# A second attention that also does the scales, the choice of experts and the normalised rows, in three portions of batches

## The reference

```
h = concat(patch_embedding(x), txt)                       # 32 x 96 x 192
h = h + attention12(layernorm(h))                         # 12 heads
h = h + soft_moe(layernorm(h))                            # 64 slots, fc1 768, gelu, fc2
h = h + attention1(layernorm(h))                          # 1 head, rotary q and k, causal
h = h + moe(layernorm(h))

def moe(x):            # x is flattened to 3072 x 192, 8 experts, top 2
    logits = x @ Wr
    topw, topi = top_k(logits, 2);  topw = softmax(topw)
    hidden = relu(x @ W1[e] + b1[e])                      # 192 -> 768
    y = hidden @ W2[e] + b2[e]                            # 768 -> 192
    return sum over the two experts of topw * y
```

## Time and profile before

| | us |
|---|---|
| median of 3 runs | 986.27 (982.88 to 988.9) |
| profiled execution | 982.65 |
| its span, first to last instruction | 980.9 |
| TensorE busy | 790.7 (81%) |
| VectorE busy | 546.9 (56%) |
| ScalarE busy | 437.7 (45%) |
| GpSimd busy | 301.3 (31%) |
| mean granted TensorE clock | 0.865 of full |

### The profile page before, as it was taken

The page is one execution under the profiler, slowest core; times in us unless marked ns, Lnnn a source line. Parts: engine busy times, 40 slices in busy tenths (PEclk is TensorE's granted clock), DMA queues, the critical chain, the costliest instruction groups (busy, mean ns, idle before and its releaser), DMA issues. The chain is left out here.

```text
span 980.9 us, 22531 instructions
## 1 busy us (share of the span) xinstructions
PE 790.7 (81%) x7454; PEld 651.8 (66%) x7455; DVE 546.9 (56%) x1512; ACT 437.7 (45%) x1056; POOL 301.3 (31%) x310
## 2 busy tenths in 40 slices
PE   3489999999779866665457999964189999999993
PEld 2368888888668533333344888852189999999993
DVE  1727777777875121111172766758356666666662
ACT  4345766667453311111003798645234444444441
POOL 1321112110034000000101587620165655555552
PEclk9758999999975787777775999975589999999997
DMA  9393000000000599999608300008613333323331
GB/s 270 90 417 152 3 0 0 0 0 1 1 2 2 238 428 424 426 428 425 263 12 341 145 1 0 1 30 128 118 39 53 52 53 51 53 47 51 53 49 19
DMA packets 39784, 119.35 MB, mean 122 GB/s; under 512 B 11130, under 2 KB 30108, under 8 KB 35260
## 3 DMA queue, kind: packets, MB, share of 16 engines
q1 hardware_dynamic: 28520, 104.98, 29.2%
q0 software_dynamic: 10848, 12.76, 8.2%
q10 hardware_dynamic: 356, 0.82, 0.3%
HBM read 105.75 MB, written 12.56 MB: 121 GB/s over the span
## 5 line engine op out<-in xcount | busy, mean ns | idle before, releaser
L1741 POOL DMA_INDIRECT out_h<-x_ys,idx x55 | 87.2, 1586 | 97.7 <-ACT x_ys L1767 74.9
L1873 PE MATMUL psum<-w_pairs,x_h_hi 128*128 x330 | 102.1, 371 | 2.0 <-DVE x_h_lo L1801 1.1
L1875 PE MATMUL psum<-w_pairs,x_h_lo 128*128 x330 | 82.6, 250 | 0.0
L1801 DVE TENSOR_TENSOR x_h_lo<-psum,x_h_hi 128x384 fp32r<-128x384 f32 x110 | 56.2, 553 | 41.9 <-ACT x_h_hi L1762 41.9
L1767 ACT ACTIVATE x_ys<-x_ys,x_cw 128x192 f32<-128x192 f32 x55 | 25.1, 456 | 98.3 <-DVE x_ys L1812 98.3
L1762 ACT ACTIVATE x_h_hi<-psum 128x384 fp32r<-128x384 f32 x110 | 48.0, 489 | 41.6 <-PE psum L1862 41.6
L1873 PEld LDWEIGHTS psum<-w_pairs,x_h_hi 128*128 128x128 f32 x330 | 61.9, 188 | 4.2 <-issue 4.2
L1875 PEld LDWEIGHTS psum<-w_pairs,x_h_lo 128*128 128x128 f32 x330 | 62.9, 191 | 0.0
L1728 POOL DMA_INDIRECT x_xg<-xtab,idx x55 | 55.3, 1005 | 16.6 <-issue 14.6
L478 POOL TENSOR_SCALAR a_xn<-flat,rstd,nmr 96x192 f32<-96x192 f32 x32 | 16.1, 502 | 136.9 <-PE psum L609 136.8
L1115 PE MATMUL psum<-flat,m_yT 64*32 64x384 f32 x576 | 38.0, 609 | 24.8 <-issue 23.5
(11 more groups left out here) (290 smaller groups left out, 2189.4 us busy)
## 6 DMA issues: line engine op xcount, KB each, us to landing
flat<-in_slot_w SPq DMA_DIRECT2D x24, 2304.0 KB, 28.6
flat<-in_moe_w SPq DMA_DIRECT2D x1, 10752.0 KB, 28.6
ring_last<-in_slot_w SPq DMA_DIRECT2D x4, 2304.0 KB, 33.6
m_y<-in_slot_w SPq DMA_DIRECT2D x4, 2304.0 KB, 31.3
flat<-in_x_patches SPq DMA_DIRECT2D x4, 1536.0 KB, 15.1
out_h<-flat SPq DMA_DIRECT2D x1, 2304.0 KB, 12.2
xtab<-flat SPq DMA_DIRECT2D x4, 576.0 KB, 11.8
ytab<-f_y2g SPq DMA_DIRECT2D x28, 48.0 KB, 28.1
```

The costliest lines, as they stand in the source:

```text
L1741: pool.indirect_dma_start(out=A["out"][:, :], out_offset=bass.IndirectOffsetOnAxis(ap=g.idx[:, i:i + 1], axis=0), in_=ys[:, i % 2, :], in_ ...
L1801: v.tensor_tensor(h_lo[:, 3 * n:3 * n + 3, :], b_hT[n], h_hi[:, 3 * n:3 * n + 3, :].bitcast(F32), ALU.subtract).then_inc(s_hl, 1)
L1873: pe.matmul(b_y[u % 2], h_hi[:, k, :], g.w_pairs[:, :, k, bass.ds(e, 1), :].rearrange("p two a d -> p two (a d)"), start=(k == 0), stop=False)
L1875: mm = pe.matmul(b_y[u % 2][:, 1, :], h_lo[:, k, :], g.w_pairs[:, 1, k, bass.ds(e, 1), :].rearrange("p a d -> p (a d)"), start=False, stop ...
```

## The change

In `attention1` every stage keeps its place; `residual` now adds into `g.h` directly, so `hn`, `keep` and its copy are gone. The batches are divided into three portions, 0 to 15, 16 to 27 and 28 to 31. When the statistics of a portion are complete, new stages follow with lags 6 to 10 behind its last batch: `variance` and `scales` (on VectorE, with `root` on ScalarE between them: logarithm and exponential and a Newton step in place of square root and reciprocal), `first_choice`, `second_choice` and `gate_weights` (VectorE, with `ratio` on ScalarE). GpSimd normalises the rows in place (`normalise`, two batches per step for the first portion, three for the second, four for the last) instead of ScalarE in `route`. SyncE writes output and table in eight groups of four batches. The column sums of the router's weights are made at the start. The loops of VectorE and TensorE are written out (`few_steps` for `steps`).

`route` keeps the counts, places and lists. There GpSimd makes the low parts of all eight late pieces; ScalarE makes each high part when its group of the table is written. `expert_tiles` no longer has the late pieces, and its first matmul waits for all of them.

```diff
+            def store_h(n):
+                part = slice(4 * n, 4 * n + 4)
+                sp.wait_ge(s_res, part.stop)
+                sp.dma_start(out_rows[:, part, :], g.h[:, part, :]).then_inc(s_h[n], 16)
+            def store_x(n):
+                part = slice(4 * n, 4 * n + 4)
+                sp.wait_ge(s_xo, part.stop)
+                sp.dma_start(tab_rows[:, part, 0:D], g.h[:, part, :]).then_inc(g.s_tab[n], 16)
+                sp.dma_start(tab_rows[:, part, D:DK], g.h[:, part, 2 * 64:D]).then_inc(g.s_tab[n], 16)
+                sp.wait_ge(s_gates, chunk_of[part.stop - 1] + 1)
+                sp.dma_start(tab_rows[:, part, DK:DK + 3], gates[:, part, :]).then_inc(g.s_gt, 16)
+            for n in range(groups):
+                store_h(n)
+                if n >= groups - 3:
+                    store_x(2 * (n - groups + 3))
+                    store_x(2 * (n - groups + 3) + 1)
+            store_x(groups - 2)
+            store_x(groups - 1)
...
+                v.scalar_tensor_tensor(g.h[:, b, :], b_o, sc[:, i, 3:4], g.h[:, b, :], ALU.mult, ALU.add).then_inc(s_res, 1)
...
+            def variance(n, c):
+                st = g.stats[:, c, :]
+                v.wait_ge(s_st, c.stop)
+                mark(v.tensor_tensor(mean[:, c], st[:, :, 1], st[:, :, 4], ALU.add))
+                mark(v.tensor_tensor(half_diff[:, c], st[:, :, 1], st[:, :, 4], ALU.subtract))
+                link(v.tensor_tensor(var[:, c], st[:, :, 2], st[:, :, 5], ALU.add))
+                mark(v.tensor_tensor(half_diff[:, c], half_diff[:, c], half_diff[:, c], ALU.mult))
+                link(v.tensor_scalar(var[:, c], var[:, c], 1.0 / D, EPS, ALU.mult, ALU.add))
+                v.scalar_tensor_tensor(var[:, c], half_diff[:, c], 0.25, var[:, c], ALU.mult, ALU.add).then_inc(s_var, 1)
+            def scales(n, c):
+                v.wait_ge(s_y, n + 1)
+                link(v.tensor_tensor(newton[:, c], y[:, c], y[:, c], ALU.mult))
+                link(v.tensor_tensor(newton[:, c], newton[:, c], var[:, c], ALU.mult))
+                link(v.tensor_scalar(newton[:, c], newton[:, c], -0.5, 1.5, ALU.mult, ALU.add))
+                link(v.tensor_tensor(g.rstd[:, c], y[:, c], newton[:, c], ALU.mult))
+                v.scalar_tensor_tensor(g.nmr[:, c], mean[:, c], -0.5, g.rstd[:, c], ALU.mult, ALU.mult).then_inc(s_nrm, 1)
...
+            def best(k, src, c):
+                size = c.stop - c.start
+                experts = g.iota[0:T, 0:NE].unsqueeze(1).broadcast_to([T, size, NE])
+                link(v.tensor_reduce(m[:, k, c], src[:, c, :], AX.X, ALU.max))
+                link(v.tensor_tensor(key[:, c, :], src[:, c, :], wide(m[:, k, c], NE), ALU.is_equal))
+                link(v.scalar_tensor_tensor(key[:, c, :], key[:, c, :], -float(NE), experts, ALU.mult, ALU.add))
+                link(v.tensor_reduce(place[:, k, c], key[:, c, :], AX.X, ALU.min))
+                link(v.tensor_tensor(g.oh[:, k, c, :], key[:, c, :], wide(place[:, k, c], NE), ALU.is_equal))
...
+            def first_choice(n, c):
+                v.wait_ge(s_gs, c.stop)
...
+                mark(v.tensor_tensor(lg[:, c, :], lg[:, c, :], wide(g.rstd[:, c], NE), ALU.mult))
+                link(v.tensor_tensor(key[:, c, :], wide(g.nmr[:, c], NE),
+                                     colsum[:, :].unsqueeze(1).broadcast_to([T, c.stop - c.start, NE]), ALU.mult))
+                link(v.tensor_tensor(lg[:, c, :], lg[:, c, :], key[:, c, :], ALU.add))
+                best(0, lg, c)
+            def second_choice(n, c):
+                mark(v.tensor_scalar(gates[:, c, 2], place[:, 0, c], float(NE), None, ALU.add))
+                link(v.scalar_tensor_tensor(lg2[:, c, :], g.oh[:, 0, c, :], -1e30, lg[:, c, :], ALU.mult, ALU.add))
+                best(1, lg2, c)
+                v.tensor_tensor(ex[:, c], m[:, 1, c], m[:, 0, c], ALU.subtract).then_inc(s_d, 1)
+                v.tensor_tensor(g.both[:, c, :], g.oh[:, 0, c, :], g.oh[:, 1, c, :], ALU.add).then_inc(g.s_both, 1)
...
+            def gate_weights(n, c):
+                v.wait_ge(s_ex, n + 1)
+                link(v.tensor_scalar(c0[:, c], ex[:, c], 1.0, None, ALU.add))
+                link(v.reciprocal(c0[:, c], c0[:, c]))
+                link(v.tensor_tensor(gates[:, c, 0], ex[:, c], c0[:, c], ALU.mult))
+                v.tensor_tensor(gates[:, c, 1], c0[:, c], gates[:, c, 0], ALU.subtract).then_inc(s_gates, 1)
...
+            few_steps(B, [(residual, 5), (gate_copy, 7), (statistics, 5), (inverse, 4), (rotate, 2), (soften, 3),
+                          (per_chunk(variance), 6), (per_chunk(scales), 7), (per_chunk(first_choice), 8),
+                          (per_chunk(second_choice), 9), (per_chunk(gate_weights), 10)], UNROLL)
...
-            def keep(b, i):
-                item(pool, s_res, b)
-                pool.tensor_copy(g.h[:, bass.ds(b, 1), :], hn[:, i, :].unsqueeze(1)).then_inc(s_keep, 1)
...
+            def normalise(at, i):
+                for b in turns[at] if at in turns else ():
+                    pool.wait_ge(s_nrm, chunk_of[b] + 1)
+                    pool.wait_ge(s_hTp, b + 1)
+                    pool.wait_ge(s_h[b // 4], 16)
+                    pool.tensor_scalar(g.h[:, b, :], g.h[:, b, :], g.rstd[:, b:b + 1], g.nmr[:, b:b + 1],
+                                       ALU.mult, ALU.add).then_inc(s_xo, 1)
...
-            few_steps(B, [(keep, 5), (add_parts, 2), (split_low, 1)], UNROLL)
...
+                    n, c = chunk_at[b], slice(*chunks[chunk_at[b]])
+                    item(act, s_var, n)
+                    act.activation(lnv[:, c], g.lnt[:, 2, c], ACT.Ln).then_inc(s_lnv, 1)
+                    item(act, s_lnv, n)
+                    act.activation(y[:, c], lnv[:, c], ACT.Exp, scale=-0.5).then_inc(s_y, 1)
...
+            few_steps(B, [(x_copy, 1), (r_copy, 3), (root, 7), (ratio, 10), (p_copy, 4), (h_copy, 6), (v_copy, 2), (norm_input, 0),
+                          (split_high, 0), (exponent, 3), (tail_top, 3)],
...
-            steps(pe, B, [(gate, 7), (transpose_x, 1), (project, 2), (transpose_qk, 3), (transpose_p, 4), (turn_h, 6),
-                          (project_v, 2), (score, 3), (attend, 4)])
...
+            few_steps(B, [(gate, 7), (transpose_x, 1), (project, 2), (transpose_qk, 3), (transpose_p, 4), (turn_h, 6),
+                          (project_v, 2), (score, 3), (attend, 4)], UNROLL)
...
-            sp.dma_start(A["out"][0:NTOK, :].rearrange("(b t) d -> t b d", t=T), g.h[:, :, :]).then_inc(s_h, 16)
...
+            for n in range(B // 4):
+                sp.wait_ge(g.s_tab[n], 32)
+            sp.wait_ge(g.s_gt, 16 * (B // 4))
...
+            for n, (_, full, hi, lo) in enumerate(g.late_pieces):
+                pool.wait_ge(g.s_hi, len(g.pieces) + n + 1)
+                pool.tensor_tensor(lo, full, hi.bitcast(F32), ALU.subtract).then_inc(g.s_lo, 1)
...
-            act.wait_ge(s_d, 1)
-            act.activation(ex[:, :], ex[:, :], ACT.Exp).then_inc(s_ex, 1)
...
-            act.wait_ge(s_h, 16)
-            for b in range(B):
-                act.activation(g.h[:, b, :], g.h[:, b, :], ACT.Identity, scale=g.rstd[:, b:b + 1],
-                               bias=g.nmr[:, b:b + 1]).then_inc(s_norm, 1)
-            act.wait_ge(s_tab, 11 * 16)
-            for _, full, hi, _ in g.late_pieces:
+            for n, (_, full, hi, _) in enumerate(g.late_pieces):
+                act.wait_ge(g.s_tab[n], 32)
                 act.activation(hi, full, ACT.Copy).then_inc(g.s_hi, 1)
...
-            link(v.tensor_tensor(g.lg[:, :, :], g.lg[:, :, :], wide(g.rstd[:, :], NE), ALU.mult))
...
-            pe.wait_ge(s_both, 1)
+            pe.wait_ge(s_ones, 1)
...
-                if t == NX - 1:
-                    for n in on_pool:
...
-            for n in on_vector:
-                v.wait_ge(g.s_hi, n_early + n + 1)
...
-            pe.wait_ge(g.s_lo, n_early)
+            pe.wait_ge(g.s_lo, len(g.pieces) + len(g.late_pieces))
```

## The result

| | before | after |
|---|---|---|
| median, us | 986.33 (982.88 to 988.9, 4 runs) | 1006.11 (1004.71 to 1007.9, 4 runs) |
| ratio of the times | | 1.0207, 95% interval 1.0182 to 1.0232 |
| span of the profiled execution | 980.9 | 1004.4 |
| granted clock, mean | 0.865 | 0.85 |

The changed kernel is slower: the interval of the ratio lies above 1. A second measurement of it, with other kernels on the chip, gave 1006.25 and a ratio of 1.0216 (1.0187 to 1.0245). The forecast was 1001 us, range 980 to 1009. Between the two profiled executions the difference is 23.5 us, between the medians 19.8; the forecast of +17 was made for the profiled one.

What follows compares the result with a forecast made beforehand. TensorE was taken to bound attention and expert tiles, with a nearly idle hand-over between. -7.4 us without conflict plus 24.4 of port waits gave +17: 999.7 profiled, 1003 on the median, 1001 taken, range 980 to 1009.

Steps and rivals of the forecast that it cites:

- forecast of +17: Whole kernel: -7.4 us without conflict plus 24.4 us of waits between VectorE and GpSimd, on the profiled execution.
- Routing: Block after attention: 21.0 us gained without conflict, 11.8 lost as VectorE's list chain waits for GpSimd's eight subtractions.
- The rule itself: VectorE operations with two SBUF inputs and GpSimd operations reading SBUF exclude each other for a whole instruction; +24.4 us together.
- The middle: First portion's stages in mid-attention: 5.4 us without conflict plus 6.6 of VectorE waiting for GpSimd.
- 5.4 without conflict: Middle of the attention: 3.0 us for ScalarE's root with table loads, 2.4 for VectorE's added operations.
- The tail: End of attention, portions two and three: +9.9 us of linked stages without conflict, +6.0 of waits beside GpSimd's rows.
- the +6.0 for GpSimd's rows: Attention tail: VectorE's choices wait beside GpSimd's 12 and 4 normalised rows, three quarters of which meet a waiting operation.
- Opening: Start of the expert tiles: no wait for late pieces and faster first gathers, 2.0 us gained.
- Rival 1: Routing and the choices: VectorE never waits for GpSimd or pays nothing; -7.4 us, 975 to 979; chance 0.20.
- Rival 2: VectorE waits in only one place, attention or routing; about +4.5 us, 988 to 991; chance 0.14.
- Rival 3: End of attention: SyncE's queued transfers, not the engines, hold the table; 999 to 1003 us; chance 0.04.

Runs made afterwards that it cites:

- late_back: Changed kernel with the eight late low parts moved out of routing, back to the opening of the expert tiles; 996.38 us, ratio 1.0103.
- micro: Changed kernel with a test stretch behind its end, each kind of VectorE operation beside each kind of GpSimd operation; its time is no measure.
- lo_paused: Changed kernel with GpSimd making no low parts in attention steps 21 to 25, the eight left in steps 26 to 32; 999.55 us, ratio 1.0134.
- two24: Changed kernel with two portions (24 and 8 batches) instead of three, rows three a step behind the first; 997.49 us, ratio 1.0175.
- final: Changed kernel with portions of 24 and 8 batches, late low parts at tile opening, VectorE reciprocal root, last gates in one transfer; 980.94 us, ratio 0.9961.

## Why the prediction was right

- **Routing, -21.0 without conflict, +11.8 with it.** Right: the chain grew by 12.4, and late_back took them away to within 0.1. The place was not right: the forecast let the waits begin at `pos` and fall on two-input operations, with `r_info` or `r_key` as the sign; they began 1.2 us into the chain, all eight fell on `r_e`, and five of them on copies and one-input operations. That the sum came out so near is in part luck: by the forecast's own rule those five would not have waited.
- **The rule itself.** Right that such an exclusion exists, wrong on who takes part. The forecast rested on x_mine, and for one-input operations on the row of 96x96, which is a reduction. Reductions pass; one-input scalings and copies of 8 elements do not (micro), while the scalings of one element do (L1271). The Trainium skill, "SBUF — State Buffer", section "Who interferes with whom", names besides two-input operations also copies and one-input scalings of VectorE, in modes that take the shared ports, and says that reductions never contend; the forecast used only its first part. On VectorE's side micro agrees with all three (1769, 1724 and 421 ns at most). The section also has any GpSimd instruction that reads SBUF contend with two inputs. Beside the rows, which read one tile, two inputs of 8 elements took 289 ns at most and of 256 elements 611 for 420: less than one row of 507 was lost, so there is contention, but the whole-instruction wait on which the forecast built was not measured.
- **The middle, +12.0.** Too low: +19.0 measured, 14.6 to 19.0 over three executions. The waits were sized well: one operation per burst waits until GpSimd's queue is empty, 7.2 us at the choices and weights (2.12, 2.01, 3.05) against 7.1. The 1.78 at the variance had no term. Nor had the clock, which held 636 to 642 at half speed; after lo_paused the middle was still +8.7, and two24's +9.8 has no wait either, against 5.4 without conflict. How the 3.3 us or more above 5.4 divide between the clock and ScalarE's and VectorE's own added work is open. Five batches took 6.8 to 8.1 us, not three.
- **The tail.** +9.9 without conflict was right (+9.8); the +6.0 for GpSimd's rows did not occur, because rows don't exclude. The errors of middle and tail, +7.0 and -6.1, nearly cancelled.
- **Opening, -2.0.** -0.6: the gather began 0.9 us after the block in place of 1.5, but landed 4.5 us after its start instead of 3.3. Over the seven profiles that open with the late parts already made, the end of the list to that matmul was 13.7 to 15.5 us, over the four edits that open with late pieces still to make 14.7 to 15.7, so the term is hardly to be told from nothing.
- **Rivals.** Rival 1 needed waits under 7.4 us; routing alone had 12.4. Rival 2 needed one place free; both had them. Rival 3: SyncE waited 2.0 us for the table at the start of routing, until 692.5, long before the lists ended.

The sum of +17 came from terms of which two were wrong by 6 to 7 us with opposite signs; that luck brought the number so near. The sign of the result rests on routing and the middle, which the runs bear out: late_back takes 1.0% off, lo_paused 0.7%.

## What to carry to other kernels

Before moving elementwise VectorE work under another stage, look at what GpSimd does there: beside its two-input operations on SBUF one VectorE operation per visit waited 1.4 to 3.2 us here, up to the whole queue. So count visits and not operations, and put them where GpSimd is idle, as two24 does; operations with an input in PSUM did not wait (166 ns in micro). Where TensorE runs at full rate, look also for the half clock behind a stall (0.50 in 636 to 642); what it costs has to be measured, for keeping the clock up bought nothing here that the intervals show.

## What the runs showed of the hardware that was not expected

- A VectorE operation that waited did not get its turn at GpSimd's next boundary in the attention (3.05 us over the end of an addition, two rows and a subtraction), while in routing, and in micro with the same four operations, one got in after every subtraction. What decides is open.
- GpSimd pays too (micro): its subtraction took 1.98 us beside VectorE's two-input operations over 256 elements, 1.80 beside small ones; its addition 1.17 for 0.99.
- An integer view of fp32 in a VectorE operation with multiplication and addition gave a usable first guess for the reciprocal root at 0.16 us for 96x24, without a table (final).
